# Attention and feed-forward layer on one core: the read of K's first half ahead of the fetch of Q's next weights

## What is computed

```
x = x + layernorm(attention(layernorm(x)))        # x: 2 x 1024 tokens x 512
x = x + layernorm(ffn(layernorm(x)))

attention:  qkv = silu(h @ qkv_w.T)               # 32 heads of 128
            per block of tokens, in order, with decays per head:
              out = (q k^T * diag_decay) v + (q * q_decay) kv
              kv  = kv * block_decay + (k * k_decay)^T v
            out = sigmoid(h @ gate_w.T) * norm_w * rmsnorm(out)
            return out @ out_w.T
ffn:        (silu(h @ gate.T) * (h @ up.T)) @ down.T, integer weights with scales
```

## Time and profile before

| | us |
|---|---|
| median of 3 runs (lowest, highest) | 2727.16 (2718.60, 2730.34) |
| the profiled execution | 2721.68 |
| its span, first to last instruction | 2719.5 |
| busy in the span: TensorE matmul | 2443.0 |
| GpSimd | 1635.7 |
| VectorE | 1383.9 |
| ScalarE | 1126.0 |
| mean granted clock of TensorE, share of full | 0.951 |

### The profile page before, as it was taken

How to read it: one execution, slowest core, us unless ns; L and a number is a source line. 1 busy time by engine, 2 the same in 40 slices (tenths; PEclk the granted TensorE clock), 3 DMA queues, 4 the chain that set the end, 5 groups by cost and what they waited for, 6 DMA issues and landing times.

```text
span 2719.5 us, 38204 instructions
## 1 busy us (share of the span) xinstructions
PE 2443.0 (90%) x12256; PEld 2061.5 (76%) x12256; DVE 1383.9 (51%) x2454; ACT 1126.0 (41%) x1666; POOL 1635.7 (60%) x1311
## 2 busy tenths in 40 slices
PE   4799999999999999999999999999999998689996
PEld 3677777777777777777877777777777777568884
DVE  5545555555555555545444544444445445544447
ACT  6533344444344443334443444444444343543333
POOL 4666666666666666656666666666666664534344
PEclk8899999999999999999999999999999999899998
DMA  3533333333333333353333332333333334100101
GB/s 116 194 109 116 116 116 110 107 105 111 115 115 106 111 114 102 116 203 130 105 105 104 104 104 95 101 102 99 96 101 104 104 104 148 67 24 29 41 23 62
DMA packets 145541, 281.09 MB, mean 103 GB/s; under 512 B 20560, under 2 KB 86096, under 8 KB 143184
## 3 DMA queue, kind: packets, MB, share of 16 engines
q1 hardware_dynamic: 139440, 269.39, 30.6%
q10 hardware_dynamic: 6048, 11.01, 1.2%
HBM read 199.60 MB, written 80.74 MB: 103 GB/s over the span
## 4 chain that ended last, share of the span: by engine, by line
PE 49%; DMA 12%; issue 11%; POOL 10%; ACT 6%; DVE 6%; SPq 3%; ACTq 0%; POOLq 0%; DVEq 0%
PE proj L1752 32%; PE yp L1752 8%; DMA kv_tok<-k_blocks 8%; PE sc L1795 4%; DMA k_blocks<-pd 4%; POOL w_lo L554 3%; SPq L370 3%; POOL w_lo L547 2%; PE sc L1808 2%; PE sc L1818 2%; POOL h_lo L686 2%; PE sc L1821 2%; ACT kd L901 1%; DVE pd L1340 1%; ACT sq L908 1%
## 5 line engine op out<-in xcount | busy, mean ns | idle before, releaser
L1752 PE MATMUL proj<-xb,w_hi 128*128 128x512 f32 x3584 | 1199.7, 417 | 183.1 <-DVE vf L1306 149.6
L1752 PEld LDWEIGHTS proj<-xb,w_hi 128*128 128x128 f32 x3584 | 681.3, 199 | 328.5 <-DVE vf L1306 162.3
L1752 PE MATMUL proj<-xb,w_lo 128*128 128x512 f32 x1792 | 726.6, 405 | 0.0
L554 POOL TENSOR_TENSOR w_lo<-ws,w_hi 128x1024 fp32r<-128x1024 f32 x128 | 307.1, 2400 | 258.2 <-ACT w_hi L854 258.2
L1752 PEld LDWEIGHTS proj<-xb,w_lo 128*128 128x128 f32 x1792 | 353.3, 197 | 81.0
L1387 DVE TENSOR_TENSOR g<-sc,g 128x512 f32<-128x512 f32 x128 | 88.5, 692 | 482.7 <-ACT sq L908 482.7
L569 POOL TENSOR_TENSOR qd<-q,table 128x512 f32<-128x512 f32 x128 | 162.9, 1284 | 203.3 <-ACT q L894 203.3
L901 ACT ACTIVATE kd<-kv_tok,table 128x512 f32<-128x512 f32 x128 | 85.4, 714 | 418.4 <-DMA kv_tok<-k_blocks 418.4
L547 POOL TENSOR_TENSOR w_lo<-raw,w_hi 128x768 fp32r<-128x768 f32 x128 | 235.7, 1842 | 4.5 <-ACT w_hi L848 1.6
L560 POOL TENSOR_TENSOR ow_lo<-kv_tok,ow_hi 128x1024 fp32r<-128x1024 f32 x32 | 76.4, 2388 | 251.3 <-ACT ow_hi L862 251.3
L1394 DVE TENSOR_TENSOR y<-yp,y 128x512 f32<-128x512 f32 x240 | 164.7, 686 | 96.1 <-PE yp L1752 94.1
(11 more groups left out here) (161 smaller groups left out, 4220.7 us busy)
## 6 DMA issues: line engine op xcount, KB each, us to landing
raw<-w_attn SPq DMA_DIRECT2D x128, 512.0 KB, 3.6
k_blocks<-pd SPq DMA_DIRECT2D x64, 512.0 KB, 3.5
kv_tok<-k_blocks SPq DMA_DIRECT2D x256, 128.0 KB, 3.3
v_blocks<-vf SPq DMA_DIRECT2D x64, 512.0 KB, 2.6
kv_tok<-v_blocks SPq DMA_DIRECT2D x256, 128.0 KB, 2.8
kv_tok<-w_out SPq DMA_DIRECT2D x32, 512.0 KB, 4.3
check<-w_ints ACTq DMA_DIRECT2D x42, 256.0 KB, 3.4
table<-tables SPq DMA_DIRECT2D x32, 258.0 KB, 3.2
```

Of the source, the lines that this page charges most:

```text
L554: pool.tensor_tensor(w_lo[:, slot, S_1:S_4 + 1], ws[:, :, :, :], w_hi[:, slot, S_1:S_4 + 1].bitcast(F32), ALU.subtract).then_inc(wlo_s_don ...
L1752: last = pe.matmul(psum, s, m, start=start and n == 0, stop=n == len(terms) - 1, skip_group_check=more)
```

## The change

In SyncE's list for a window the read of K's half 0 is placed ahead of the fetch of Q's weights for the next window. All windows written by `window()` are touched: 1 to 30. Window 0 has a list of its own, and window 31 fetches no further weights.

```
@@ -413,9 +413,9 @@
                 k_write(w, 1)
                 k_read(w, 1)
                 k_write(w, 0)
+                k_read(w, 0)
                 if next_weights:
                     weights(w + 1, QQ, pair + 1 if not isinstance(pair, int) else (pair + 1) % PAIRS)
-                k_read(w, 0)
                 v_write(w, 1)
                 v_write(w, 0)
                 if second_batch:
```

## The result

The changed kernel took 2533.19 us (median of 4 runs, 2529.04 to 2536.85) against 2725.00 for the kernel before beside it: a ratio of 0.9297, 95% interval 0.9271 to 0.9322. Predicted were 2538, range 2500 to 2590. The profiled execution took 2529.04 us, its span is 2527.0, TensorE's mean granted clock 0.975 (before 0.951).

The account below looks back on a forecast made before the run. The bound was taken to be K's late read, held by an unrelated wait and stalling TensorE at VV 3. 2721.68 - 149.6 - 69 + 30 = 2533 us, plus 5.5 for the median: 2538, range 2500 to 2590.

Parts of the forecast that it names:

- The origin: K's read, queued behind the Q-weight fetch that waits for GpSimd's w_lo, stalls TensorE at VV 3; it moves 9.2 us forward.
- What is removed: TensorE's whole stop at VV 3 and the slow clock after it: 218.6 us together, 7.29 per window.
- The clock's part: After the stop at VV 3, 18 matmuls take 6.40 us instead of 4.10: 2.30 us per window, 69 us.
- The new waits: TensorE waits 0.65 us at GG 2 and 0.35 at KK 3: 1.0 us per window, 30 us in all.
- the first estimate: From window 14's times, TensorE waits about 0.4 us at GG 2 for GpSimd's g_lo and ScalarE's copy.
- I take the whole stop away: At VV 3 in all 30 windows: 149.6 us of idleness and 69 us of slow clock vanish.
- A: TensorE alone is the bound, new waits below 0.3 us per window: 2508 to 2517 us; chance 0.12.
- B: GpSimd's row or V's path through memory takes 2.5 to 5 us per window: 2584 to 2659 us; chance 0.08.
- C: TensorE's clock falls at short stops too; one slow stretch per window gives 2607 us; chance 0.05 for one or two.
- the case of three slow stretches per window: New stops at GG 2, KK 5 and KK 3 each bring a slow stretch: 2745 us; chance 0.02.
- D: Nothing happens, as the read's own waits or another chain hold `kd`: 2727 us; chance 0.03.
- The contention of GpSimd with VectorE: Shared SBUF interfaces slow GpSimd's row before GG 2 by 2%: 0.2 us per window, 6 us, inside the range.

Follow-up runs that it names:

- experiment 1: The changed kernel with the wait for GpSimd's w_lo of G left ahead of both read and fetch, so only the 512 KB fetch changes sides: 2646.49 us, ratio 0.9732.
- experiment 2: The changed kernel with one more wait ahead of the early read, for GpSimd's w_lo of G's sums, which ends 1.8 us sooner: 2562.69 us, ratio 0.9426.
- experiment 5: The changed kernel with GpSimd's four sums of K's next weights (2.9 us) moved behind both g_lo: 2510.13 us, ratio 0.9227.

## Why the prediction was right

*The origin.* The read was held by the wait of the instruction ahead of it; experiments 1 and 2 show that with graded doses: with the read 13.1, 12.5, 10.7 and 4.0 us after its write, TensorE stood 5.0, 3.1, 1.4 and 0 us at VV 3. The read went 4.06 us after its write in window 14 as window 31 had it (3.99), and ScalarE's wait for the reads fell to 116.6 us, where some 115 were forecast.

*What is removed.* 7.29 us per window were taken for granted. A full-speed window turned out to be 62.67 us (experiment 5), so the windows before held 7.56 us of loss in the first batch and 6.97 in the second, on average 7.26.

*The clock's part.* 2.30 us per window was a little too much. It took 6.40 us as the mean of two windows and 4.10 from elsewhere in the list; over all 30 stops the 18 matmuls took 6.28 us on average, and 4.2 in the same place with the clock up (experiment 2), so 2.06. The busy time of TensorE fell by 25.5 us in 13 windows, 1.96 each, and by 2.16 in the second batch. Against experiment 5 the windows before held 2.30 us more busy time on average, the very figure, but the changed kernel keeps 0.37 us of it in the first batch and 0.11 in the second at a granted clock of 1.00, so that part is not the clock's.

*The new waits.* 1.0 us per window were expected, at GG 2 and at KK 3. They stand there, but smaller and uneven: 63.48 - 62.67 = 0.81 us in the first batch, of which 0.45 is idleness, and 0.14 in the second. KK 3 has only three stops in the first batch, of 0.17 to 0.28 us, where 0.35 in every window was taken. For GG 2 alone window 14 had given 0.4 and window 31 1.0; the stops were 0.2 to 0.6 us in windows 2 to 14, so the first estimate was the better. (It took the mean stop of 4.99 us; window 14's own was 4.89, by which the estimate would be 0.3.) That the second batch has hardly any was not foreseen. The traces show where the difference begins: counted from the marks, GpSimd's row of work (its first `qd`, which waits for ScalarE's q) starts later in the first batch, at 48.6 against 48.2 us before the change, at 49.4 against 48.2 after it, and at 48.4 against 47.9 in experiment 5, which has no stops. About half a microsecond of this is there in every kernel, and stops of this size would be hidden by it; no run was made to test that, and what makes ScalarE later in the first batch stays open.

*What was missed.* The sum counted all 30 windows alike, at 7.29 - 1.0 = 6.29 us. The 26 steady periods gave 176.4 us, 12.9 more than that, because the new waits were smaller. The three at the change of batches gave 12.2, 6.6 less: where TensorE no longer stood at VV 3 it ran ahead to other waits, for the activations, for V's late read and, for 1.57 and 1.40 us, at GG 2, and two of these stops brought the lower clock with them. Window 0 to 1 and what lies outside gave 3.9, 2.4 less. So the total, 192.5 against 188.6, is nearer than its terms: two errors of 13 and 9 us partly cancelled. The terms that failed in size are "1.0 us per window" and, for the middle, "I take the whole stop away".

*The rivals.* A (TensorE alone is the bound) is nearly so in the second batch and was reached by moving one more step (2510.13 us). B and C did not come; for C, the case of three slow stretches per window, the new stops under 1 us in the steady windows brought none: the clock stands at 1.00 in both long stretches. Frequent small idle pieces, from which by the Trainium skill (TensorE: Matmul & The Clock Gate, "A second HAM failure mode") the clock swung between its two levels in another kernel, did not do so here: one stop of 0.2 to 0.6 us per window left it up. It fell behind longer single stops, 21 of 30 in experiment 1. D is refuted. The contention of GpSimd with VectorE, weighed for an extra 6 us, is hardly to be seen: g_lo's pair takes 2.53 us after as before, and of GpSimd's instructions in the steady windows `qd` grew most, from 1.278 to 1.293 us on average.

## What to carry to other kernels

In an engine's queue, look at what each wait holds besides its own instruction: here the wait for a buffer whose next content nobody needed yet delayed a read that all waited for, by 9 us in every window. The stop itself (TensorE at VV 3) was several steps away from it, behind ScalarE's `kd` and square and VectorE's gate and `keep_s3`. One window that lacks the instruction (the last) already showed what would happen without it. After such a gain the next bound is close: 2.9 us of work moved to a later place on GpSimd made the steady windows pure TensorE time.

## What the runs showed of the hardware

A 512 KB fetch issued ahead of four 128 KB reads on the same queue made these land about 1 us later (5.25 against 4.20 us from issue to use). And stops of TensorE of nearly the same length, 2.71 and 2.73 us, left the granted clock at 2.4 GHz in one case and brought it down to 1.2 GHz in the other; of 25 stops under 2 us in the second experiment one (1.89 us) was followed by the lower clock. The changed kernel's stop of 1.75 us at 1152.80 was followed by it too. A stop shortened from 5 us to 1 is therefore worth more than the idleness it saves: in experiment 2 TensorE's stops at VV 3 fell by 107.5 us and the time by 156.
